# A graph layer on one core: second stage's first loads later, last read-backs into other buffers, sums in front of squares, and a plain tile behind a correction

## The chip, the core and the metric

The kernel runs on one core of a Trainium2 chip. The metric is the device time of one execution in microseconds. TensorE is called PE in the profile, VectorE DVE, ScalarE ACT, GpSimd POOL, and SyncE, which issues most transfers, SP.

## The reference

50,000 nodes with 512 features each, and 75,000 edges: 12,500 drawn ones in both directions and a loop at every node. A node's neighbours are averaged, two products and a bias give `h`, `h` is normalised over all nodes (a batch normalisation), added to `x` after a relu, and each row is normalised once more. All in float32.

```python
summed = jax.ops.segment_sum(x[src], dst, num_segments=n)
cnt = jax.ops.segment_sum(jnp.ones((src.shape[0],), x.dtype), dst, num_segments=n)
aggr = summed / jnp.maximum(cnt, 1.0)[:, None]
h = aggr @ W_l.T + b_l + x @ W_r.T
mu = jnp.mean(h, axis=0)
var = jnp.mean(jnp.square(h - mu), axis=0)
h_norm = (h - mu) * jax.lax.rsqrt(var + EPS) * gamma + beta
...
x = _layernorm(x + relu(h_norm), axis=-1)
```

## The kernel before

Rows are handled in groups of 640, five tiles of 128 rows: 78 whole groups (0 to 77) and a last one, 78, of 80 rows. There are two stages.

**Stage one** writes `h` to `h_scratch` in HBM. Most nodes have no neighbour but themselves, so `h` is first `x` times the sum of both weight matrices. A *plain tile* is that product for 128 rows: `product` (L524 to L526), twelve matmuls, three for each of four slices of the contraction, because every float32 operand is split into a high and a low part. ScalarE makes `x_hi` from `raw` (L728), VectorE `x_lo` (L1045), ScalarE copies the product from bank `pd` to `h_out` (L735), SyncE stores a group (L379).

Nodes with real neighbours need a correction. They are packed 128 to a half, two halves to a *pair*; there are U = 78 pairs. For pair `u`, GpSimd gathers rows (`xe`, `xn`, `xf`, L1331), VectorE forms differences `dd` (L1094), TensorE spreads the extra rows (L613, L614), transposes a difference (L621) and multiplies it by the left weights into bank `pz` (`correction`, L627 to L629, twelve matmuls). ScalarE makes `dT_hi` (L786), VectorE `dT_lo` (L1100), ScalarE scales the product into `zz` (`copy_z`, L793), and GpSimd adds it to `h_scratch` by a scatter (L1379). Both halves use the one bank `pz`, so correction 1 waits until `zz` of half 0 has been copied.

All engines walk the same list of *turns*, u = -2 to 81. A turn holds pair `u`, four or five plain tiles (`tiles_at(u)`; none from turn 75 on), the making of one-hots and slots for pair `u + 2` (`fill_slots`, L600, L603), and sums: group `u - 3` is read back from `h_scratch` into `hs` (`load_sums`, L392, two buffers), VectorE adds it to `acc1` (`take_sums`, L1109), ScalarE squares it in place (L799) and VectorE adds the squares to `acc2` (`take_squares`, L1116). Among the turns 2 to 74, 34 have four tiles. The order in an engine is the order of the code; engines meet at semaphores.

SyncE waits in `load_sums` for the stores of the group, for the scatters of pair `g + 1` (at most 77), and for the squares that last used the buffer. In turn 74, behind the last store, `load_early` issues the loads of the second stage's first three blocks (KEPT = 3).

At the end of stage one TensorE sums the accumulators over the partitions (`sum_columns`, L643) and VectorE and ScalarE turn them into a scale and an offset for each feature (`bn_ready`).

**Stage two** reads `h` and `x` again in blocks of 640 rows, into nine places (NB2 = 9) that lie over the buffers of stage one. GpSimd scales `h` (L1402), VectorE adds the offset (L1243) and forms `y` with its sum (L1248), ScalarE takes squares about the mean (L881) and normalises (`normalise`, L891), SyncE stores (L493). Block `k` is normalised behind the squares of block `k + 1`. `raw` and `x_lo` lie under place 0, `x_hi` under place 1, `h_out` under place 2.

## Time and profile before

| | us |
|---|---|
| median of three runs | 2595.24 |
| lowest, highest | 2591.77, 2596.50 |
| the profiled execution, own time | 2596.68 |
| its span in the trace | 2594.9 |
| TensorE busy | 1757.6 (68% of the span) |
| VectorE busy | 1956.6 (75%) |
| ScalarE busy | 1471.8 (57%) |
| GpSimd busy | 1456.2 (56%) |

The numbers below come from the one profiled execution. Busy shares are means over two stages that have little in common, so they say little; what an engine waits for, and in which stretch, says more. The ends of matmuls are modelled, and one begins before the last is shown as over; the distance between starts is what counts.

### The profile page before, as it was taken

To read this page: it belongs to the slowest core of one execution; us is meant where nothing else is said; L and a number is where in the kernel's file an instruction comes from. 1 tells how busy PE (TensorE), PEld (TensorE's weight loads), DVE (VectorE), ACT (ScalarE), POOL (GpSimd) and SP (SyncE) were. 2 spreads that over 40 slices of the span, in tenths; PEclk is the share of its full clock that TensorE was granted. 3 is DMA by queue.
4 is the path that set the end of the run, shared out by engine and by line. 5 is a ranking of instruction groups with operands and counts; after the bars stand their busy time and mean duration, and the time that the engine had idled before them with its cause. 6 is when DMAs were issued, how large, how long until landed. Compare 5 with 4: busy or idle time off the path is not lost.

```text
span 2594.9 us, 29629 instructions
## 1 busy us (share of the span) xinstructions
PE 1757.6 (68%) x9404; PEld 1415.7 (55%) x9404; DVE 1956.6 (75%) x3451; ACT 1471.8 (57%) x2847; POOL 1456.2 (56%) x700
## 2 busy tenths in 40 slices
PE   7899999999999999999999999996400000000000
PEld 5778778878877887787778778874200000000000
DVE  6745878888877888888788888785688666666666
ACT  4333455545554554454445445542389988888887
POOL 5354555555555555555565555554196655555564
PEclk9999999999999999999999999997755555555555
DMA  5466878887888878888788878877599999999998
GB/s 184 139 211 206 260 250 266 277 253 246 257 263 255 258 246 259 258 255 264 234 262 271 255 243 253 280 240 247 163 410 426 426 426 426 426 412 414 421 421 344
DMA packets 125533, 752.89 MB, mean 290 GB/s; under 512 B 20809, under 2 KB 20809, under 8 KB 65726
## 3 DMA queue, kind: packets, MB, share of 16 engines
q1 hardware_dynamic: 70464, 617.84, 62.1%
q0 software_dynamic: 53664, 132.51, 20.7%
q8 instruction: 77, 1.26, 0.2%
q10 hardware_dynamic: 1246, 0.60, 0.1%
q14 instruction: 82, 0.67, 0.1%
HBM read 515.32 MB, written 246.22 MB: 293 GB/s over the span
## 4 chain that ended last, share of the span: by engine, by line
PE 33%; DMA 32%; issue 9%; DVE 9%; ACT 8%; POOL 7%; SPq 0%; POOLq 0%; ACTq 0%; DVEq 0%
DMA out<-hx 19%; PE pd L524 7%; PE pd L526 7%; PE pd L525 7%; DMA xn<-x,gi 5%; DMA xf<-x,gi 5%; PE pz L627 3%; PE pz L629 3%; PE pz L628 3%; ACT hx L881 3%; POOL xn L1331 2%; ACT hx L891 2%; DVE x_lo L1045 2%; POOL xf L1331 2%; DMA hs<-h_scratch 1%
## 5 line engine op out<-in xcount | busy, mean ns | idle before, releaser
L524 PE MATMUL pd<-wc_hi,x_hi 128*128 128x512 f32 x1564 | 628.8, 402 | 34.8 <-DVE wc_lo L922 17.3
L1379 POOL DMA_INDIRECT h_scratch<-zz,si x156 | 308.8, 1979 | 564.5 <-ACT zz L793 506.9
L735 ACT ACTIVATE h_out<-pd 128x512 f32<-128x512 f32 x391 | 233.6, 597 | 672.3 <-PE pd L526 652.1
L526 PE MATMUL pd<-wc_hi,x_lo 128*128 128x512 f32 x1564 | 614.6, 393 | 0.0
L525 PE MATMUL pd<-wc_lo,x_hi 128*128 128x512 f32 x1564 | 612.9, 392 | 0.0
L1402 POOL TENSOR_TENSOR hx<-hx,scale_b 128x2560 f32<-128x2560 f32 (+2 forms) x91 | 439.4, 4838 | 293.3 <-DMA hx<-h_scratch 251.8
L524 PEld LDWEIGHTS pd<-wc_hi,x_hi 128*128 128x128 f32 x1564 | 295.4, 189 | 98.5 <-issue 29.9
L526 PEld LDWEIGHTS pd<-wc_hi,x_lo 128*128 128x128 f32 x1564 | 295.2, 189 | 64.7
L525 PEld LDWEIGHTS pd<-wc_lo,x_hi 128*128 128x128 f32 x1564 | 295.9, 189 | 57.9
L1331 POOL DMA_INDIRECT xn<-x,gi x156 | 264.9, 1698 | 47.7 <-issue 47.7
L881 ACT ACTIVATE hx<-hx,nm 128x512 f32<-128x512 f32 x391 | 277.1, 710 | 2.8
L891 ACT ACTIVATE hx<-hx,nr,rs 128x512 f32<-128x512 f32 x385 | 278.6, 798 | 0.0
L627 PE MATMUL pz<-wl_hi,dT_hi 128*128 128x512 f32 x624 | 256.5, 411 | 28.9 <-ACT zz L793 20.3
L1331 POOL DMA_INDIRECT xf<-x,gi x156 | 248.7, 1594 | 47.6 <-issue 47.3
L1079 DVE SCALAR_TENSOR_TENSOR xf<-xn,ndeg,xf 128x512 f32<-128x512 f32 x156 | 114.9, 746 | 185.8 <-issue 140.3
L799 ACT ACTIVATE hs<-hs 128x512 f32<-128x512 f32 x391 | 219.1, 621 | 51.1 <-DVE acc L1109 51.1
L628 PE MATMUL pz<-wl_lo,dT_hi 128*128 128x512 f32 x624 | 247.4, 396 | 0.0
L629 PE MATMUL pz<-wl_hi,dT_lo 128*128 128x512 f32 x624 | 246.4, 395 | 0.0
L728 ACT ACTIVATE x_hi<-raw 128x640 fp32r<-128x640 f32 (+1 forms) x316 | 214.1, 724 | 40.7 <-DMA raw<-xT_whole 40.6
L1109 DVE TENSOR_TENSOR acc<-acc,hs 128x2560 f32<-128x2560 f32 (+1 forms) x79 | 220.1, 2786 | 21.7 <-DMA hs<-h_scratch 21.7
L1116 DVE TENSOR_TENSOR acc<-acc,hs 128x2560 f32<-128x2560 f32 (+1 forms) x79 | 220.2, 2787 | 16.0 <-ACT hs L799 16.0
L1045 DVE TENSOR_TENSOR x_lo<-raw,x_hi 128x640 fp32r<-128x640 f32 x280 | 209.4, 808 | 14.7 <-ACT x_hi L728 14.7
(221 smaller groups left out, 2855.0 us busy)
## 6 DMA issues: line engine op xcount, KB each, us to landing
raw<-xT_whole SPq DMA_DIRECT2D x78, 1280.0 KB
h_scratch<-h_out SPq DMA_DIRECT2D x78, 1280.0 KB
hs<-h_scratch SPq DMA_DIRECT2D x78, 1280.0 KB
hx<-x SPq DMA_DIRECT2D x78, 1280.0 KB, 20.7
hx<-h_scratch SPq DMA_DIRECT2D x77, 1280.0 KB, 15.4
out<-hx SPq DMA_DIRECT2D x77, 1280.0 KB, 18.0
xn<-x,gi POOLq DMA_INDIRECT x156
xf<-x,gi POOLq DMA_INDIRECT x156
```

What stands on the lines that cost most here:

```text
L524: pe.matmul(pd[i][0:n, :], hi, wc["hi"][:, kc, :], start=kc == 0, stop=False)
L525: pe.matmul(pd[i][0:n, :], hi, wc["lo"][:, kc, :], start=False, stop=False)
L526: last = pe.matmul(pd[i][0:n, :], lo, wc["hi"][:, kc, :], start=False, stop=kc == KC - 1)
L627: pe.matmul(out_bank[0:n, :], hi, wl["hi"][:, kc, :], start=kc == 0, stop=False)
L628: pe.matmul(out_bank[0:n, :], hi, wl["lo"][:, kc, :], start=False, stop=False)
L629: last = pe.matmul(out_bank[0:n, :], lo, wl["hi"][:, kc, :], start=False, stop=kc == KC - 1)
L881: act.activation(hb[i][0:n, t, :], xb[i][0:n, t, :], ACT.Square, bias=nm2[0:n, k % 4, t:t + 1], accum_out=ssq2[0:n, k % 4, t:t + 1]).then_ ...
L891: act.activation(hb[i][0:n, t, :], xb[i][0:n, t, :], ACT.Identity, bias=nr2[0:n, k % 4, t:t + 1], scale=rs2[0:n, k % 4, t:t + 1]).then_inc ...
L1045: dve.tensor_tensor(x_lo[:, b, kc, 0:n], raw[:, b, kc, 0:n], x_hi[:, b, kc, 0:n].bitcast(F32), ALU.subtract).then_inc(s_xld, 1)
L1331: return pool.indirect_dma_start(out=table if scatter else out, out_offset=by if scatter else None, in_=out if scatter else table, in_offs ...
L1379: pool.indirect_dma_start(out=h_dram[:, :], out_offset=by, in_=zz[:, h, :], in_offset=None, bounds_check=N + 2 * P - 1, oob_is_err=True, c ...
L1402: pool.tensor_tensor(hb[i][0:n, a:b], hb[i][0:n, a:b], scale_b[0:n].unsqueeze(1).to_broadcast([n, b - a, D]), ALU.mult).then_inc(s_mul, 1)
```

## The change

Five things, in the order of the program.

- SyncE no longer issues the first loads of stage two in turn 74. It issues two blocks (EARLY2 = 2) in turn 77, once all gathers of the last pair have landed, and four more (up to KEPT = 6) after the last read-back, once TensorE has finished all corrections. Places are handed out in another order, so that the place over `h_out` comes seventh.
- The read-backs of groups 76 and 77 go into the two halves of `h_out`, and each of the last three has a semaphore of its own; they no longer wait for squares.
- From turn 78 on VectorE takes the sums of a group ahead of the squares of the group before.
- In turns with four plain tiles TensorE does the fourth behind correction 0 and not ahead of it.
- In stage two block 0 is normalised at once, ahead of the squares of block 1.

```diff
@@ the places
-        KEPT = 3
+        EARLY2, KEPT = 2, 6
         hx = s2("hx", [P, NB2, 2, TG, D], F32)
-        hb = [hx[:, i, 0] for i in range(NB2)]
-        xb = [hx[:, i, 1] for i in range(NB2)]
+        places = (0, 1, 3, 4, 5, 6, 2, 7, 8)
+        hb = [hx[:, i, 0] for i in places]
+        xb = [hx[:, i, 1] for i in places]
@@ new
+        def sums_of(g):
+            return h_out[:, g % 2] if isinstance(g, int) and G - 2 <= g < G else hs[:, g % 2]
+
+        def read_back(g):
+            return s_sl_end[g - G + 2] if isinstance(g, int) and g >= G - 2 else s_sl[g % 2]
@@ SyncE, load_sums
-                if g >= 2:
-                    sp.wait_ge(s_a2, g - 1)
-                sp.dma_start(part_of(hs[:, b], g), group_of(h_dram, g)).then_inc(s_sl[b], 16)
+                if G - 2 <= g < G:
+                    sp.wait_ge(s_st[0], stored(G))
+                    sp.wait_ge(s_st[1], stored(G - 1))
+                elif g >= 2:
+                    sp.wait_ge(s_a2, g - 1 if g < G else G - 3)
+                sp.dma_start(part_of(sums_of(g), g), group_of(h_dram, g)).then_inc(read_back(g), 16)
@@ SyncE, the turns
                         if t == tiles_in(g) - 1:
                             after_group(g, g % 2)
-                        if g == G:
-                            load_early()
                     if sums_at(u + 1) is not None:
                         load_sums(sums_at(u + 1))
+                    if u == U - 1:
+                        sp.wait_ge(s_ge, 16 * U)
+                        for h in range(2):
+                            sp.wait_ge(s_gn[h], 16 * U)
+                            sp.wait_ge(s_gf[h], 16 * U)
+                        sp.wait_ge(s_dm, TG * G + 1)
+                        load2(0, EARLY2)
+                sp.wait_ge(s_z, 2 * U)
+                load2(EARLY2, KEPT)
             sp.wait_ge(s_done, 1)
-            for k in range(KEPT, NB2 - 1):
-                load2_h(k)
-                load2_x(k)
+            load2(KEPT, NB2 - 1)
@@ TensorE, the turns
-                    plain(3)
+                    if len(tiles) == TG:
+                        plain(3)
                     if a is not None:
                         correction(a, 0)
-                    plain(4)
+                    plain(3 if len(tiles) < TG else 4)
                     if u + 2 < U:
                         fill_slots(u + 2)
@@ ScalarE, stage two (VectorE's invert in the same way)
-                if k >= 1 and not by_vector(k - 1):
+                if k == 0:
+                    normalise(0)
+                if k >= 2 and not by_vector(k - 1):
                     normalise(k - 1)
@@ VectorE, the turns
-                    if sums_at(u - 1) is not None:
+                    if u < U and sums_at(u - 1) is not None:
                         take_squares(sums_at(u - 1))
...
                     if sums_at(u) is not None:
                         take_sums(sums_at(u))
+                    if u >= U:
+                        take_squares(sums_at(u - 1))
```

TensorE in turn 66, which has four tiles, from transposition 1 on (bank `p7`), before. `pd0` is the fourth plain tile, `pz` with `dT_hi0` correction 0, `psl` the slots, `pz` with `dT_hi1` correction 1; of each block of twelve matmuls the first stands here.

```order
L621 MATMUL p7<-ident,dd 128x128 [waits dT_lo_ready,differences_ready]
L621 MATMUL p7<-ident,dd 128x128 x3
L524 MATMUL pd0<-wc_hi,x_hi 128x512 [waits h_copied]
...
L627 MATMUL pz<-wl_hi,dT_hi0 128x512 [waits z_copied,dT_lo_ready]
...
L600 MATMUL psl<-vals,hot 128x6 [waits slots_copied,one_hots_built]
L600 MATMUL psl<-vals,hot 128x6 x12
L603 MATMUL psl<-valsx,hotx 128x4 x10
L627 MATMUL pz<-wl_hi,dT_hi1 128x512 [waits z_copied,dT_lo_ready]
```

The same stretch of TensorE after the change.

```order
L636 MATMUL p7<-ident,dd 128x128 [waits dT_lo_ready,differences_ready]
L636 MATMUL p7<-ident,dd 128x128 x3
L642 MATMUL pz<-wl_hi,dT_hi0 128x512 [waits z_copied,dT_lo_ready]
...
L539 MATMUL pd0<-wc_hi,x_hi 128x512 [waits h_copied]
...
L615 MATMUL psl<-vals,hot 128x6 [waits slots_copied,one_hots_built]
L615 MATMUL psl<-vals,hot 128x6 x12
L618 MATMUL psl<-valsx,hotx 128x4 x10
L642 MATMUL pz<-wl_hi,dT_hi1 128x512 [waits z_copied,dT_lo_ready]
```

Correction 0 and the fourth tile have changed places; nothing else in the turn has.

ScalarE in the same turn, after the change, from `dT_hi` of half 1 on. Apart from line numbers it reads so before too: the copy of the fourth tile (`h_out<-pd0`) stands ahead of `xe_hi` and of `zz` of correction 0.

```order
L802 ACTIVATE dT_hi1<-p7 128x512 [waits z_summed,differences_transposed]
L751 ACTIVATE h_out<-pd0 128x512 [waits h_summed]
L796 ACTIVATE xe_hi<-xe 128x512 [waits extras_spread,extras_gathered]
L809 ACTIVATE zz<-pz,wgt 128x512 [waits z_added0,weights_ready,z_summed]
L815 ACTIVATE hs<-hs 128x512 [waits sums_taken]
L815 ACTIVATE hs<-hs 128x512 x2
L809 ACTIVATE zz<-pz,wgt 128x512 [waits z_added1,weights_ready,z_summed]
```

Nothing moved on this engine, while one of the things it waits for did.

SyncE's queue before, from the last group's store in turn 74 on: three blocks of `hx`, then the read-backs into `hs` of groups 72 to 74 (four more stand behind them).

```order
L379 DMA h_scratch<-h_out 80x512 [waits h_copied]
L399 DMA hx<-h_scratch 128x2560 [waits h_stored0,h_stored1,h_copied,h_summed]
L403 DMA hx<-x 128x2560
L399 DMA hx<-h_scratch 128x2560
...
L392 DMA hs<-h_scratch 128x2560 [waits z_added1,squares_taken,z_added0,h_stored0]
L392 DMA hs<-h_scratch 128x2560 [waits z_added1,squares_taken,z_added0,h_stored1]
```

SyncE's queue after, from the read-back of group 74 on.

```order
L406 DMA hs<-h_scratch 128x2560 [waits z_added1,squares_taken,z_added0,h_stored0]
L406 DMA hs<-h_scratch 128x2560 [waits z_added1,squares_taken,z_added0,h_stored1]
L413 DMA hx<-h_scratch 128x2560 [waits rows_gathered1,neighbours_gathered1,neighbours_gathered0,h_summed,rows_gathered0,extras_gathered]
L417 DMA hx<-x 128x2560
...
L406 DMA h_out<-h_scratch 128x2560 [waits h_stored0,z_added1,h_stored1,z_added0] x2
L406 DMA hs<-h_scratch 80x512 [waits z_added1,squares_taken,z_added0,h_stored0]
L413 DMA hx<-h_scratch 128x2560 [waits z_summed]
L417 DMA hx<-x 128x2560
```

The loads of `hx` have moved behind four of the seven read-backs (two blocks) and behind all seven (four blocks).

## Rows read from the trace of the kernel before

**Rows 1.** The page, busy tenths and GB/s in 40 slices of the span.
```profile
PE   7899999999999999999999999996400000000000
...
GB/s 184 139 211 206 260 250 266 277 253 246 257 263 255 258 246 259 258 255 264 234 262 271 255 243 253 280 240 247 163 410 426 426 426 426 426 412 414 421 421 344
```

**Rows 2.** TensorE's waits, 450 to 1740 us: us in total, times, longest.
```profile
PE pz L627 <- ACT zz L793: 12.1, 28, 1.5
...
PE pe L613 <- issue: 1.0, 6, 0.2
```

**Rows 3.** Timeline of TensorE, turn 66: start, us, what, wait before it.
```profile
1591.47 0.48 PE L524 MATMUL pd<-wc_hi,x_hi 128*128 128x512 f32 x1
...
1594.32 0.39 PE L627 MATMUL pz<-wl_hi,dT_hi 128*128 128x512 f32 x1
...
1598.07 0.47 PE L627 MATMUL pz<-wl_hi,dT_hi 128*128 128x512 f32 x1 [0.30 <-ACT zz L793]
...
1600.89 0.39 PE L613 MATMUL pe<-xe_hi,spread 128*128 128x512 f32 x1
```

**Rows 4.** Timeline of ScalarE, turn 66.
```profile
1588.60 1.36 ACT L728 ACTIVATE x_hi<-raw 128x640 fp32r<-128x640 f32 x2
...
1594.52 0.60 ACT L735 ACTIVATE h_out<-pd 128x512 f32<-128x512 f32 x1 [2.12 <-PE pd L526]
1595.01 0.62 ACT L780 ACTIVATE xe_hi<-xe 128x512 fp32r<-128x512 f32 x1
1597.24 0.69 ACT L793 ACTIVATE zz<-pz,wgt 128x512 f32<-128x512 f32 x1 [1.60 <-PE pz L629]
```

**Rows 5.** Timelines, turns 17, 19, 66: fourth tile's start, low part of difference 0.
```profile
552.75 0.48 PE L524 MATMUL pd<-wc_hi,x_hi 128*128 128x512 f32 x1
...
554.93 0.68 DVE L1100 TENSOR_TENSOR dT_lo<-px,dT_hi 128x512 fp32r<-128x512 f32 x1
...
595.89 0.48 PE L524 MATMUL pd<-wc_hi,x_hi 128*128 128x512 f32 x1
...
596.71 0.68 DVE L1100 TENSOR_TENSOR dT_lo<-px,dT_hi 128x512 fp32r<-128x512 f32 x1
...
1590.48 0.69 DVE L1100 TENSOR_TENSOR dT_lo<-px,dT_hi 128x512 fp32r<-128x512 f32 x1 [0.47 <-ACT dT_hi L786]
```

**Rows 6.** TensorE around two waits; stretches with granted clock, DMA share, GB/s last.
```profile
792.23 0.68 PE L627 MATMUL pz<-wl_hi,dT_hi 128*128 128x512 f32 x1 [1.50 <-ACT zz L793]
...
796.64 0.40 PE L613 MATMUL pe<-xe_hi,spread 128*128 128x512 f32 x1
...
1025.82 0.47 PE L627 MATMUL pz<-wl_hi,dT_hi 128*128 128x512 f32 x1 [1.52 <-ACT zz L793]
...
780.00:800.00 20.00, 18.50 (x99) 15.03 (x98) 13.23 (x18) 8.52 (x15) 13.09 (x6) 0.91 0.82 272
1015.00:1035.00 20.00, 18.48 (x104) 14.84 (x103) 15.67 (x23) 9.84 (x18) 11.04 (x7) 1.00 0.90 280
1580.00:1602.00 22.00, 21.70 (x120) 17.84 (x119) 19.68 (x36) 11.77 (x21) 11.13 (x7) 1.00 0.87 279
```

**Rows 7.** The seam: chain of waits (first row), timelines, one stretch.
```profile
1774.70 29.31 DMA hs<-h_scratch
...
1804.04 2.83 DVE L1109 TENSOR_TENSOR acc<-acc,hs 128x2560 f32<-128x2560 f32 x1 [21.69 <-DMA hs<-h_scratch]
...
1809.97 1.56 POOL L1379 DMA_INDIRECT h_scratch<-zz,si  x1 [16.41 <-DVE si L1069]
...
1844.44 0.33 SPq L392 DMA_DIRECT2D hs<-h_scratch  x1
...
1862.21 2.71 ACT L799 ACTIVATE hs<-hs 128x512 f32<-128x512 f32 x5 [5.63 <-DVE acc L1109]
...
1869.06 0.69 DVE L1116 TENSOR_TENSOR acc<-acc,hs 80x512 f32<-80x512 f32 x1 [0.69 <-ACT hs L799]
...
1910.00:1920.00 10.00, 0.00 (x0) 0.00 (x0) 9.97 (x32) 9.90 (x23) 10.00 (x3) 0.50 0.95 365
```

More of the change, by code:

```diff
@@ L265, in bass_sage_batchnorm_residual_layernorm_kernel @@
         s_sl = [sem(f"h_loaded{b}") for b in range(2)]
+        s_sl_end = [sem(f"h_end_loaded{i}") for i in range(3)]
         s_a1, s_sq, s_a2 = sem("sums_taken"), sem("squares_ready"), sem("squares_taken")
@@ L403, in load2_x, with load2 @@
                 sp.dma_start(part_of(xb[i], k), group_of(x, k)).then_inc(s_x2[i], 16)
-            def load_early():
-                sp.wait_ge(s_dm, TG * G + 1)
-                sp.wait_ge(s_ev, TG * G + 1)
-                sp.wait_ge(s_st[0], stored(G))
-                sp.wait_ge(s_st[1], stored(G - 1))
-                for k in range(KEPT):
+            def load2(first, end):
+                for k in range(first, end):
                     load2_h(k)
@@ L466, in _ @@
                 correct(G)
-                load_early()
+                sp.wait_ge(s_done, 1)
+                load2(0, KEPT)
             with sp.Else():
@@ L798, in square @@
                     act.wait_ge(s_a1, g + 1)
-                act.activation(hs[0:n, g % 2, t, :], hs[0:n, g % 2, t, :], ACT.Square).then_inc(s_sq, 1)
+                act.activation(sums_of(g)[0:n, t, :], sums_of(g)[0:n, t, :], ACT.Square).then_inc(s_sq, 1)
             act.wait_ge(s_flag, 1)
@@ L1104, in take_sums @@
                 n, t = rows_in(g), tiles_in(g)
-                dve.wait_ge(s_sl[g % 2], stored(g))
+                dve.wait_ge(read_back(g), stored(g) if g < G - 2 else 16)
                 dve.wait_ge(s_clear, 1)
@@ L1108, in take_sums @@
                     dve.wait_ge(s_a1, g)
-                dve.tensor_tensor(acc1[0:n, 0:t], acc1[0:n, 0:t], hs[0:n, g % 2, 0:t], ALU.add).then_inc(s_a1, 1)
+                dve.tensor_tensor(acc1[0:n, 0:t], acc1[0:n, 0:t], sums_of(g)[0:n, 0:t], ALU.add).then_inc(s_a1, 1)
             def take_squares(g):
@@ L1115, in take_squares @@
                     dve.wait_ge(s_a2, g)
[L1116 removed]
+                dve.tensor_tensor(acc2[0:n, 0:t], acc2[0:n, 0:t], sums_of(g)[0:n, 0:t], ALU.add).then_inc(s_a2, 1)
             dve.wait_ge(s_flag, 1)
@@ L1275, in _ @@
                     sum_y(k, t)
-                if k >= 1:
+                if k == 0:
+                    invert(0)
+                if k >= 2:
                     invert(k - 1)
```

5 lines of the change are left out of this document (1 added, 4 removed).

## The prediction, made before the kernel had run

> **What bounds the kernel now.** I read the page first: its forty slices show TensorE at nine tenths or more up to about 1770 us and then nothing, and the transfers at 410 to 426 GB/s from about 1870 us to the end [rows 1]. So there are two stages and a seam. In stage one TensorE sets the pace: between 450 and 1740 us its waits are six kinds, 28 us in 1290, the largest the 28 waits for the scaled copy `zz` with 12.1 us and the least 1.0 us [rows 2]. In stage two the transfers set the pace. The seam, 1770 to 1915 us, is a chain of waits with no engine busy. A microsecond saved on ScalarE or VectorE is worth nothing in either stage, but a microsecond in which TensorE stands still in stage one is lost whole. I therefore looked first for what the change does to TensorE's order, which its title does not mention, and then at the seam.
>
> **Part one: the fourth tile behind the first correction.** A turn `u` of the loop handles one pair of corrections and the next four or five plain tiles; 34 turns have four, 43 have five. Five-tile turns keep their order. In a four-tile turn TensorE now does transposition 1, correction 0, the fourth tile, the slots, correction 1, where it did the fourth tile before correction 0. ScalarE's order stays: copy of the fourth tile (`h_out`), `xe_hi`, `zz` of correction 0. Correction 1 needs that `zz`, since both use bank `pz`. Before, the fourth tile's copy was long done when correction 0 ended; now the copy waits for a product that ends later than correction 0, and `zz` stands behind it.
>
> Worked out on turn 66. Before, the fourth tile starts at 1591.47, where transposition 1 ends, correction 0 at 1594.32, and correction 1 at 1598.07, after 0.30 of waiting [rows 3]. ScalarE takes up `zz` at 1597.24, when correction 0 is out, and TensorE goes on 0.83 later [rows 3, 4]. After, the two blocks change places, so the fourth tile ends where correction 0 ended. ScalarE starts `h_out` at 1597.24, needs 0.49 for it (1594.52 to 1595.01) and about 0.54 for `xe_hi` (0.62 less the tenth by which neighbours overlap) [rows 4], takes up `zz` at 1598.27, and correction 1 starts at 1599.10: **1.03 us later**. Times 34 turns: 35 us. VectorE's work on `xe` is delayed alike and stays just in time for the next turn.
>
> When the fourth tile is a group's tile 1 or 2, two `x_hi` conversions follow its copy and also stand ahead of `zz`: 1.36 us for the pair [rows 4], 1.26 after overlap, in 14 turns: 18 us.
>
> Correction 0 now comes straight behind transposition 1 and needs `dT_lo` of half 0. In turn 66 that ends at 1591.17 and the transposition at 1591.47: no wait [rows 3, 5]. In turn 17 VectorE has a group's `x_lo` ahead of it and finishes at 555.61, while the fourth tile starts at 552.75: 2.9 us, which that tile covered before. In turn 19 it is 597.39 against 595.89: 1.5 us [rows 5]. Read off so, 19 turns have such a lateness and together 40 us.
>
> Sum 93 us. The 28 old waits above their usual 0.30 (12.1 less 28 times 0.30, [rows 2]) are already in the old times and come off: 89. Some is recovered: a TensorE that waits lets VectorE and the gathers catch up, so the other five kinds of waits, 16 us, fall away, and turn 17's lateness shrinks a little. I allow 20 us for both; the rest is **+69**. Bounds: 53 us if no `dT_lo` is ever late and 89 with no recovery.
>
> **The clock.** The new standstills are longer than the old. At 792.23 TensorE had waited 1.50 us with only the tiny slot products before it; the granted clock of that stretch is 0.91, and the correction that follows takes until 796.64, 4.41 us, where turn 66's takes 2.82 [rows 3, 6]. At 1025.82 it had waited 1.52 us and the clock stayed at 1.00 [rows 6]. So a fall to the lower level (1.2 instead of 2.4 GHz) costs 1.6 us and comes at some waits of 1.5 us. The change makes 53 standstills: 34 at correction 1 of about 1.4 us, 2.7 in the fourteen turns with `x_hi`, and 19 at correction 0. I count 24 falls, the long ones and some of the short: **+38**. From below it is 0, from above 85 (53 times 1.6).
>
> The Trainium skill bears on this ("TensorE: Matmul & The Clock Gate", section "A second HAM failure mode: psum-queue depth-cycling"): short idles between groups of matmuls that come often enough make the clock swing between half and full. By that rule already the small waits of before should do it; the stretch of 22 us around turn 66 with its 0.30 shows a clock of 1.00 [rows 6], so here size decides and not number. By the rule the clock would fall at nearly every new wait; that is the second rival.
>
> **Part two: the seam.** Before, SyncE issues six loads of 1.31 MB ahead of the read-back of group 72, which is issued at 1774.70 and lands 29.31 us later; VectorE stands 21.69 us [rows 7]. After, that read-back goes first and VectorE needs it at 1782.4, when it is long there: the stall goes. What is late next is the pair chain. `zz` of pair 75 waited for VectorE's sums through ScalarE's squares, so its scatter went out at 1809.97 [rows 7]. Without that, and with `xe` gathered through a free queue, correction 1 of pair 75 ends near 1792 and its scatter goes at about 1793, an estimate between 1791 and 1795: 17 us earlier. From there to the last scatter the steps stay as they were.
>
> Two blocks (5.2 MB, 12.3 us at 426 GB/s) are now loaded between the last gathers and the last scatters. They share the transfer engines with the scatters, which must have landed before the last three read-backs are issued. Cost between 0 and 6 us; I take 2. A read-back was issued at 1844.44 when the last scatter had landed [rows 7]. From there came rounds of 8.3 us, ScalarE's 2.71 of squares and 5.63 of waiting for VectorE [rows 7]: sums 2.8, squares 2.7, squares added 2.8, each behind the one before. With three buffers the read-backs follow one another and the next sums run while ScalarE squares: 5.5 us a round. From 1844.44 to the end of the last addition, 1869.75 [rows 7], was 25.3 us, and is now about 5 for landing plus 15.4. But the column sums of the squares wait for group 77's squares, which are now 1.3 us closer to the end, so 3.6 us remain. Seam: 17 plus 3.6 less 2, **-19**.
>
> **Part three: stage two.** Three more blocks are there early, and block 0 is normalised and stored about 8 us sooner. I cost both at nothing. The store that starts the steady stream is block 1's, behind GpSimd's block 2, which hangs on the batch statistics alone. Before it, the transfers already had a gap (0.95 busy, 365 GB/s at 1910 to 1920, [rows 7]); all nine blocks were in. Loads that come earlier make that gap longer, and only that. If I were wrong, the bound is three blocks of two loads, 18 us at 426 GB/s.
>
> **Sum.** The profiled execution's span is 2594.9, its own time 2596.7, the median 2595.2. Span: 2594.9 + 69 + 38 - 19 = 2682.9; with the 0.3 us by which the median stands above the span, **2683**.
>
> **Rivals.**
> 1. The waits come, the clock does not fall (for: 1025.82; against: 792.23). 2595.2 + 69 - 19 = 2645. Chance 0.22.
> 2. The clock falls at nearly every wait, as the skill's rule would have it, and nothing is recovered: 2595.2 + 89 + 70 - 19 = 2735. Chance 0.08. The mechanism is the same wait; the price is 1.6 us each, from the correction at 792.23.
> 3. Not slower: TensorE does not set stage one's pace but VectorE and the gathers behind it do, so the moved tile's wait falls into time that was idle anyway, while the 12.1 us of old `zz` waits are gone. 2595.2 - 12 - 19 = 2564. Against it stands that TensorE had so few waits [rows 2]. It decides in favour of faster once more than 88 of the 107 us are absorbed. Chance 0.07.
> 4. Absorbed in part, so that waits and seam cancel within 5 us: chance 0.03.
>
> **How the numbers follow.** The forecast has 0.60. Its own range is 2655 to 2715: 53 to 80 us of waits, 20 to 60 of clock, 13 to 25 of seam. To leave out no more than two in ten the range takes in most of rival 1 and stops short of rivals 2 and 3: 2632 to 2725. A measurement can tell about 0.2%, 5 us. Slower 0.60 + 0.22 + 0.08 = 0.90, same 0.03, faster 0.07.
>
> **What would show it.** Right: in the trace of after the waits of TensorE at `pz` for ScalarE's `zz` go from 12 us to 50 or more, a wait for `dT_lo` of some 30 us appears, four-tile turns take 1 to 5 us longer, the granted clock dips below 1.00 in many stretches, and stage two starts 70 to 110 us later, though the distance from the last four-tile turn to the first normalised block shrinks by about 19 us. Wrong: if stage one ends before about 1780 us, rival 3 holds; if it ends near 1840 with the clock at 1.00, rival 1; if stage two lasts less than before by over 5 us, part three was wrong.

## The result and the profile after

| | before | after |
|---|---|---|
| median, us | 2595.87 | 2705.25 |
| lowest, highest of four runs each | 2591.77, 2598.57 | 2700.10, 2709.44 |
| span of the profiled execution | 2594.9 | 2698.1 |
| TensorE's waits on `pz`, 450 to 1740 us | 13.3 | 87.8 |
| start of turn 75, the first without tiles | 1772.91 | 1893.56 |
| from there to the end of the span | 822.0 | 804.5 |

The change makes the kernel slower by 4.2% (ratio 1.0422, 95% interval 1.0402 to 1.0442). The two last rows tell the story in two numbers: stage one became 120.7 us longer, and seam and stage two together 17.5 us shorter. The forecast was 2683, with 107 and 19 for the two.

On the page of after, busy tenths, granted clock and GB/s in 40 slices, TensorE's row has eights where it had nines [rows 1]:

```profile
PE   7899989989999999899899999999510000000000
...
PEclk9999999999999999999999999999755555555555
...
GB/s 177 156 193 224 251 188 263 263 196 241 236 243 239 223 247 253 243 230 256 235 223 237 257 220 228 263 244 205 216 363 420 426 426 426 426 426 426 413 421 342
```

A tenth is too coarse for the clock. The stretch that [rows 2] cover, with the granted clock and the DMA share behind the busy times (it was 1.00 and 0.82 before), and TensorE's waits in the same stretch (us in total, times, longest):

```profile
450.00:1740.00 1290.00, 1199.23 (x6442) 977.79 (x6441) 980.45 (x1403) 591.14 (x1029) 659.57 (x397) 0.97 0.77 238
...
PE pz L642 <- ACT zz L809: 46.4, 26, 2.6
PE pz L642 <- DVE dT_lo L1118: 41.4, 15, 4.4
PE p L636 <- DVE dd L1112: 2.4, 4, 0.8
PE pd L539 <- issue: 0.4, 1, 0.4
```

The six kinds of waits of [rows 2] have become four. The first went from 12.1 to 46.4 us and a second, for `dT_lo`, from 1.2 to 41.4. All others together fell from 14.4 to 2.8: while TensorE stands still, what it would else have waited for gets ready. (The same 1290 us hold fewer turns in after, so the true growth is larger; the table by turns below has it.)

**Turn 66, the `zz` wait.** TensorE's timeline, to be held against [rows 3], then ScalarE's, against [rows 4]:

```profile
1701.16 0.48 PE L642 MATMUL pz<-wl_hi,dT_hi 128*128 128x512 f32 x1
...
1704.01 0.39 PE L539 MATMUL pd<-wc_hi,x_hi 128*128 128x512 f32 x1
...
1708.77 0.57 PE L642 MATMUL pz<-wl_hi,dT_hi 128*128 128x512 f32 x1 [1.30 <-ACT zz L809]
...
1713.18 0.40 PE L628 MATMUL pe<-xe_hi,spread 128*128 128x512 f32 x1
```
```profile
1706.93 0.60 ACT L751 ACTIVATE h_out<-pd 128x512 f32<-128x512 f32 x1 [4.83 <-PE pd L541]
1707.42 0.62 ACT L796 ACTIVATE xe_hi<-xe 128x512 fp32r<-128x512 f32 x1
1707.94 0.68 ACT L809 ACTIVATE zz<-pz,wgt 128x512 f32<-128x512 f32 x1
```

Correction 0 is at 1701.16, the fourth tile at 1704.01. ScalarE, idle for 4.83 us, copies that tile as soon as it is there, then `xe_hi`, and only then `zz`, on which correction 1 waits 1.30 us in place of 0.30. The forecast had 1.03 more; it is 1.00. Then the clock: from the second product behind the wait on they follow one another at 0.43 us instead of 0.23, and the correction takes 4.41 us (1708.77 to 1713.18) where turn 66 had taken 2.82 [rows 3].

**Turn 41, the `dT_lo` wait.** VectorE's timeline, then TensorE's first product of correction 0 and the tile that follows it:

```profile
1121.58 0.75 DVE L1097 SCALAR_TENSOR_TENSOR xf<-xn,ndeg,xf 128x512 f32<-128x512 f32 x1 [6.08 <-issue]
...
1127.93 3.04 DVE L1063 TENSOR_TENSOR x_lo<-raw,x_hi 128x640 fp32r<-128x640 f32 x4
1130.89 2.81 DVE L1134 TENSOR_TENSOR acc<-acc,hs 128x2560 f32<-128x2560 f32 x1
1133.63 0.68 DVE L1118 TENSOR_TENSOR dT_lo<-px,dT_hi 128x512 fp32r<-128x512 f32 x1
```
```profile
1134.36 0.50 PE L642 MATMUL pz<-wl_hi,dT_hi 128*128 128x512 f32 x1 [3.43 <-DVE dT_lo L1118]
...
1138.65 0.54 PE L539 MATMUL pd<-wc_hi,x_hi 128*128 128x512 f32 x1
```

`x_lo` of a whole group (3.04) and the addition of the squares (2.81) stand ahead of `dT_lo` on VectorE. That was so before, and the fourth tile covered it. But VectorE is also late as a whole: it stood 6.08 us ahead of `xf`. The profile names no releaser there; the instruction waits for gathered rows. In turn 40, GpSimd's last gather and the read-back that SyncE issues, in after and then in before:

```profile
1110.04 0.33 SPq L406 DMA_DIRECT2D hs<-h_scratch  x1
...
1111.13 3.63 POOL L1353 DMA_INDIRECT xf<-x,gi  x1 [0.30 <-issue]
```
```profile
1038.21 1.17 POOL L1331 DMA_INDIRECT xf<-x,gi  x1 [0.30 <-issue]
...
1042.06 0.33 SPq L392 DMA_DIRECT2D hs<-h_scratch  x1
```

Before, the gather went out 9.58 us into turn 40 and 3.85 ahead of the read-back; after, 12.01 into the turn and 1.09 behind it, and it occupied GpSimd for 3.63 us in place of 1.17. The turn itself is shorter, 21.65 us in place of 23.00; TensorE had waited 0.85 us in it and no longer does.

**All turns.** I added up the distance between the starts of neighbouring turns, TensorE's waits in them, and, as time lost to the lower clock, the excess over 2.85 us of each correction or tile that took more than 0.6 us longer than that (each is one fall). In turns 3 to 74:

| | turns | total before | after | waits before | after | lost to the clock before | after | falls |
|---|---|---|---|---|---|---|---|---|
| four tiles | 33 | 647.3 | 798.1 | 14.4 | 115.0 | 1.6 | 45.3 | 1, then 28 |
| five tiles | 39 | 878.3 | 844.4 | 19.8 | 0.0 | 3.1 | 0.0 | 2, then 0 |

The five-tile turns, which the change leaves alone, became 34 us shorter; that is the recovery. Of the 151 us that the four-tile turns grew, 100.6 are waits and 43.7 clock.

**The seam of after.** In order of time: GpSimd's scatter that answers to the one at 1809.97 in [rows 7], SyncE's first early load, the last scatter, the last read-backs, the first sums that they bring, GpSimd's first work of stage two.

```profile
1912.80 1.56 POOL L1401 DMA_INDIRECT h_scratch<-zz,si  x1 [2.02 <-ACT zz L809]
...
1934.54 0.33 SPq L413 DMA_DIRECT2D hx<-h_scratch  x1
...
1942.54 1.56 POOL L1401 DMA_INDIRECT h_scratch<-zz,si  x1 [2.27 <-ACT zz L809]
...
1953.16 0.83 SPq L406 DMA_DIRECT2D h_out<-h_scratch  x2
...
1958.56 2.83 DVE L1127 TENSOR_TENSOR acc<-acc,h_out 128x2560 f32<-128x2560 f32 x1 [12.90 <-DMA h_out<-h_scratch]
...
1987.39 3.71 POOL L1424 TENSOR_TENSOR hx<-hx,scale_b 128x512 f32<-128x512 f32 x3 [43.29 <-DVEq L1256]
```

Counted from the start of turn 75, the scatter of [rows 7] at 1809.97 stood at 37.06 us and stands at 19.24, 17.8 earlier. The last scatter came 17.8 earlier too (66.76, now 48.98), the last read-backs 11.9 earlier (71.53, now 59.60), and GpSimd's stage two 16.0 earlier (109.78, now 93.83). The read-backs wait for the last scatter to land: 4.8 us before, 10.6 now.

### The profile page after: what moved, and what is told of

Its sections match the earlier page's. It is cut to its first block, busy times and chain, and to the rows that moved or that the text cites. A ratio compares the mean times of both kernels' runs of the same rounds, so it can differ in the third digit from the quotient of the medians.

```text
span 2698.1 us, 29630 instructions
## 1 busy us (share of the span) xinstructions
PE 1792.7 (66%) x9404; PEld 1451.1 (54%) x9404; DVE 1958.2 (73%) x3451; ACT 1467.0 (54%) x2847; POOL 1432.6 (53%) x700
## 3 DMA queue, kind: packets, MB, share of 16 engines
q8 instruction: 77, 1.26, 0.2%
## 4 chain that ended last, share of the span: by engine, by line
PE 44%; DMA 28%; ACT 9%; DVE 7%; issue 7%; POOL 4%; SPq 0%; POOLq 0%; ACTq 0%; DVEq 0%
DMA out<-hx 18%; PE pd L539 8%; PE pd L541 8%; PE pd L540 8%; PE pz L642 5%; PE pz L644 5%; PE pz L643 5%; DMA xn<-x,gi 3%; ACT hx L897 3%; ACT hx L907 2%; DMA raw<-xT_whole 2%; DMA xf<-x,gi 2%; DVE x_lo L1063 2%; DMA h_scratch<-zz,si 1%; ACT zz L809 1%
## 5 line engine op out<-in xcount | busy, mean ns | idle before, releaser
L1401 POOL DMA_INDIRECT h_scratch<-zz,si x156 | 317.2, 2034 | 734.1 <-ACT zz L809 677.8
L642 PE MATMUL pz<-wl_hi,dT_hi 128*128 128x512 f32 x624 | 274.5, 440 | 122.7 <-ACT zz L809 63.8
L1353 POOL DMA_INDIRECT xn<-x,gi x156 | 247.0, 1583 | 47.7 <-issue 47.4
L644 PE MATMUL pz<-wl_hi,dT_lo 128*128 128x512 f32 x624 | 265.4, 425 | 0.0
L643 PE MATMUL pz<-wl_lo,dT_hi 128*128 128x512 f32 x624 | 264.6, 424 | 0.0
L815 ACT ACTIVATE hs<-hs 128x512 f32<-128x512 f32 x381 | 213.7, 623 | 7.5 <-DVE acc L1127 7.5
L1127 DVE TENSOR_TENSOR acc<-acc,hs 128x2560 f32<-128x2560 f32 (+1 forms) x77 | 214.5, 2785 | 3.4 <-DMA hs<-h_scratch 3.4
L1134 DVE TENSOR_TENSOR acc<-acc,hs 128x2560 f32<-128x2560 f32 (+1 forms) x77 | 214.6, 2786 | 0.6 <-ACT hs L815 0.5
```

The lines of the kernel that those rows point to most:

```text
L642: pe.matmul(out_bank[0:n, :], hi, wl["hi"][:, kc, :], start=kc == 0, stop=False)
L643: pe.matmul(out_bank[0:n, :], hi, wl["lo"][:, kc, :], start=False, stop=False)
L644: last = pe.matmul(out_bank[0:n, :], lo, wl["hi"][:, kc, :], start=False, stop=kc == KC - 1)
L1353: return pool.indirect_dma_start(out=table if scatter else out, out_offset=by if scatter else None, in_=out if scatter else table, in_offs ...
L1401: pool.indirect_dma_start(out=h_dram[:, :], out_offset=by, in_=zz[:, h, :], in_offset=None, bounds_check=N + 2 * P - 1, oob_is_err=True, c ...
```

## The experiments

Times are medians; the ratio is to the kernel before on the same chip, with its 95% interval. A difference between two kernels is the difference of their ratios times 2594 us, since not all ran in one session.

### The tile's place: the change without it, and it alone

```diff
  x1_order_back: the changed kernel, with
-                    if len(tiles) == TG:
-                        plain(3)
+                    plain(3)
                     if a is not None:
                         correction(a, 0)
-                    plain(3 if len(tiles) < TG else 4)
+                    plain(4)
```
x2_tile_alone is the kernel before with the same lines the other way round.

> The changed kernel, with TensorE's tiles of a four-tile turn in the order of the kernel before (fourth tile, correction 0, nothing, correction 1). Theory (the tile's new place costs about 120 us in stage one, and the seam gives about 17.5 back): 2595.9 - 17.5 = about 2578, which is 125 to 130 us under the changed kernel. In the trace the waits of the four-tile turns are near 14 us in place of 115, and the granted clock of stage one is near that of the kernel before. Rival (the loss comes from the new places of the loads and read-backs, and the tile is innocent): about 2700, as the changed kernel.

> The kernel before, with the one edit of TensorE's order: in a four-tile turn the fourth tile comes behind correction 0. Theory (the loss and the gain lie in different stages and add up): 2595.9 + 120.7 = about 2717, so slower than the changed kernel by the seam's 17 us. Rival (the tile costs nothing by itself): about 2596. A third outcome, about 2705, would say that the seam's gain was made by something in the tile's move.

x1_order_back: 2585.43, ratio 0.9970 (0.9955 to 0.9985). x2_tile_alone: 2716.06, ratio 1.0489 (1.0460 to 1.0519), where the theory said 2717. The tile's place alone makes the loss: it costs 127 us when it is put into the kernel before, and taking it out of the changed one gives 117 back. In x2's trace turn 75 begins at 1886.10, 113 us late, with 25 falls of the clock in four-tile turns. TensorE's waits of x1_order_back, 450 to 1740 us, are those of [rows 2] again:

```profile
PE pz L642 <- ACT zz L808: 14.7, 28, 2.4
...
PE pz L642 <- DVE dT_lo L1117: 1.5, 5, 0.3
```

One part missed. The seam alone was to give 17.5 us, and x1_order_back gains 7.8 (3.9 to 11.7). Its profiled span, 2578.1, has 5 of its 17 us from a stage one that happened to be shorter, and 11.6 behind the start of turn 75. What became of the rest is told with the seam, below.

### ScalarE's share: `zz` first

```diff
  x3_zz_first: the changed kernel, ScalarE's turn
-                    plain(tiles[3:4])
+                    if len(tiles) == TG:
+                        plain(tiles[3:4])
                     if pair_at(u + 1) is not None:
                         extras_high(u + 1)
                     if a is not None:
                         copy_z(a, 0)
-                    plain(tiles[4:])
+                    plain(tiles[4:] if len(tiles) == TG else tiles[3:4])
```

> The changed kernel, with one edit on ScalarE: in a four-tile turn it copies the half of z that correction 1 multiplies ahead of the fourth tile's copy, not behind it. Theory (both standstills of TensorE have a cause of their own, and the clock falls with each): the waits of correction 1 on that copy, 54 us in the sum, go; those of correction 0 on dT_lo, 44 us, stay; about half of the 28 falls of the clock (some 20 us) go with them. 2705 - 54 - 20 = about 2630, range 2615 to 2655. Rival A (the dT_lo waits shrink too, since VectorE gets its tiles sooner): under 2600. Rival B (what is taken off one wait comes back in the other, because a turn is as long as VectorE's and ScalarE's chain): above 2680.

2619.74, ratio 1.0106 (1.0076 to 1.0136), 82 us under the changed kernel. Its waits, 450 to 1740 us:

```profile
PE pz L642 <- DVE dT_lo L1119: 44.2, 16, 4.1
PE pe L628 <- DVE xe_lo L1103: 2.5, 6, 0.4
PE p L636 <- DVE dd L1113: 2.3, 6, 0.8
```

The `zz` wait has left this list and the `dT_lo` wait is where it was, 44.2 for 41.4: two waits with two causes, and the theory holds within 10 us. The falls went from 28 to 13.

It shows more: VectorE's lateness does not come from the late `zz`. In turn 41, with `zz` on time, VectorE stands at `xf` and TensorE waits for `dT_lo` no less than in the changed kernel:

```profile
1079.76 0.75 DVE L1098 SCALAR_TENSOR_TENSOR xf<-xn,ndeg,xf 128x512 f32<-128x512 f32 x1 [6.37 <-issue]
```
```profile
1092.64 0.80 PE L642 MATMUL pz<-wl_hi,dT_hi 128*128 128x512 f32 x1 [3.84 <-DVE dT_lo L1119]
```

So it is in turns 8, 19, 30, 41, 52 and 63, the turns whose fourth tile is a group's tile 0 (turn 74, the seventh, has no such wait): TensorE waits 3.8 to 5.0 us there, in after 3.4 to 4.5. Ahead of each, in both kernels, the last gather stands 1.1 us behind the read-back; in the kernel before it stands 2.4 to 3.9 ahead of it.

### The clock's share: standstills filled with work

```diff
  x4_busy_waits: the changed kernel, TensorE's turn
+                    def busy(n):
+                        for _ in range(n):
+                            pe.matmul(pe_[:], wc["hi"][:, 0, 0:P], wc["hi"][:, 0, :], start=True, stop=True)
...
+                    if len(tiles) == 4 and a is not None and tiles[3][1] in (0, 1, 2):
+                        busy(6)
                     if a is not None:
                         correction(a, 0)
...
                         fill_slots(u + 2)
+                    if len(tiles) == 4 and a is not None:
+                        busy(10 if tiles[3][1] in (1, 2) else 5)
                     if a is not None:
                         correction(a, 1)
```

> The changed kernel, with products of TensorE that nobody reads put into its standstills: 6 ahead of correction 0 in the kinds of turn that waited there, 5 or 10 ahead of correction 1. They only keep the engine working; the waits' causes are as they were. Theory (of the 120 us, about 45 are the clock falling to half after a standstill, the rest are the waits themselves): the granted clock of stage one is back near 1.00 and the time is 35 to 45 us under the changed kernel, about 2665, less what the products overrun the waits. Rival (the falls fall beside the wait and cost nothing of their own): 2705 or more.

2661.69, ratio 1.0266 (1.0245 to 1.0286), 40 us under the changed kernel with more work on TensorE, not less. ScalarE's and VectorE's orders are as they were, so the causes of the waits are too; only TensorE is busy until they end. The stretch of 450 to 1740 us, the clock third from last:

```profile
450.00:1740.00 1290.00, 1262.77 (x6831) 1025.58 (x6830) 999.98 (x1425) 604.64 (x1053) 679.30 (x407) 0.99 0.79 245
```

0.99 where the changed kernel has 0.97; in the four-tile turns 5 falls in place of 28, and 9.3 us lost in place of 45.3. So the clock is a cost of its own, some 45 us, of which 36 went here; the rest of the tile's 117 is waits. This separates the two terms of the forecast, 69 and 38.

### VectorE's share: `dT_lo` first as well

```diff
  x12_both_first: x3_zz_first, VectorE's turn
+                    if p is not None:
+                        difference_low(p, 0)
                     x_lows(1)
                     if u < U and sums_at(u - 1) is not None:
                         take_squares(sums_at(u - 1))
-                    if p is not None:
-                        difference_low(p, 0)
                     x_lows(2)
```

> x3_zz_first (the changed kernel with TensorE's new order, and z copied first), and on VectorE the low part of difference 0 taken ahead of the group's x_lo and the squares, in every turn. In x3_zz_first TensorE still waited 54 us for dT_lo and the clock fell 13 times. Theory (dT_lo of half 0 is late because x_lo and the squares stand ahead of it on VectorE, 3.0 and 2.8 us): those waits shrink to under 15 us, the falls to a few, and the time is 2620 - 40 - 15 = about 2565. Rival (VectorE itself is late in these turns, since the gathers land late, so the order inside the turn matters little): above 2600. A third outcome, x_lo now late for the next turn's tiles, would show as waits of TensorE's tiles on x_lo.

2575.58, ratio 0.9938 (0.9920 to 0.9956): 44 us under x3_zz_first. The rival said over 2600; it fell. The theory's number, 2565, is missed by 10. Its waits, 450 to 1740 us:

```profile
PE pd L539 <- issue: 14.6, 7, 2.9
PE px L636 <- DVE dd L1113: 8.1, 7, 1.7
PE pe L628 <- DVE xe_lo L1103: 5.9, 11, 0.5
PE p L636 <- DVE dd L1113: 3.7, 9, 0.8
PE pz L642 <- ACT zz L809: 0.8, 1, 0.8
```

`dT_lo` is gone from the list. With TensorE's new order and the two engines that feed it put in the same order, the four-tile turns take 637.0 us, 10 less than before the change, with no fall of the clock. The tile's new place was not wrong by itself: it was moved on one engine of three. But the five-tile turns took 886.1 us, 8 more than before, with 34.3 us of waits in place of 19.8 (on `issue` ahead of a tile, and on `dd`) and five falls in place of two, 8.5 us in place of 3.1. I tried whether VectorE's new order does that there:

```diff
  x13_four_only: x12_both_first, with
-                    if p is not None:
+                    early = len(tiles_at(u)) < TG
+                    if p is not None and early:
                         difference_low(p, 0)
...
+                    if p is not None and not early:
+                        difference_low(p, 0)
                     x_lows(2)
```

> x12_both_first, with VectorE's new order (low part of difference 0 first) in turns of fewer than five tiles alone. In x12_both_first the four-tile turns took 637 us in place of 647, but the five-tile turns 886 in place of 878, with 34 us of waits. Theory A (VectorE's order there makes them wait): the five-tile turns come down by 10 us or more and the time is about 2565. Theory B (TensorE, when it gains in the four-tile turns, runs into the loads and gathers, and gives the gain back in whatever turn follows): five-tile turns stay near 885 and the time at 2575, within 3 us.

2576.17, ratio 0.9927 (0.9914 to 0.9940). Theory B: four-tile turns 634.0, five-tile turns 889.9 with 35.9 us of waits, and the start of turn 75 at 1771.73, where it was 1769.88 in x12_both_first and 1772.91 in the kernel before. What TensorE gains in one kind of turn is handed back in the other. That loads and gathers are what it then runs into is read from the waits' names, not shown by a run of its own.

### ScalarE's order with the old order of TensorE

x8_zz_first_old_order is x1_order_back with the ScalarE diff above.

> x1_order_back, with ScalarE's copy of z for correction 1 taken ahead of the fourth tile's copy in four-tile turns. TensorE had there, in each four-tile turn, one wait of 0.30 us for that copy. Theory (TensorE's order with a tile between is right, and ScalarE's order is free to be changed): these go, 10 us in the sum, and nothing comes in their place: 2585 - 10 = about 2575. Rival (the fourth tile's copy, x_lo and with it dT_lo come later, and the 10 us are given back): 2585 or more.

2575.95, ratio 0.9930 (0.9910 to 0.9949), 10 us under x1_order_back. The number came, the reason did not. The waits of 0.30 us are still in every kind of four-tile turn (28 waits for `zz`, now 8.6 us, all near 0.30): nothing lies between the corrections but the slots, so they measure the way from one correction over the copy to the next. Two other things moved. In turns whose fourth tile is a group's tile 1, two `x_hi` conversions no longer stand ahead of `zz`; those seven turns fell from 20.98 to 19.56 us each, 10 in the sum (the traces scatter here: 20.25 in the kernel before, 20.04 in x10_both), but the five-tile turns rose by 12 and the profiled stage one kept nothing (turn 75 starts at 1770.36, in x1_order_back's profile at 1767.73). And the seam with stage two became 6 us shorter (804.3, after 810.4), which may be most of the 10 and goes with something worth seeing. In x1_order_back SyncE issues a read-back at 1762.48 and VectorE then stands 7.45 us until the gathered `xf` is there; in x8 the last tile's copy is 3.3 us later against turn 75's start, the store and the read-back behind it go out at 1768.42, and VectorE stands 2.16. The two rows of each:

```profile
1762.48 0.54 SPq L406 DMA_DIRECT2D hs<-h_scratch  x1
...
1771.74 0.75 DVE L1096 SCALAR_TENSOR_TENSOR xf<-xn,ndeg,xf 128x512 f32<-128x512 f32 x1 [7.45 <-issue]
```
```profile
1768.42 10.41 SPq L406 DMA_DIRECT2D hs<-h_scratch  x2
...
1769.07 0.75 DVE L1097 SCALAR_TENSOR_TENSOR xf<-xn,ndeg,xf 128x512 f32<-128x512 f32 x1 [2.16 <-issue]
```

The gathers had been issued alike (the last at 1760.70 in x1_order_back and 1763.31 in x8, 2.84 us each on GpSimd's queue); they landed within 8.2 us beside the read-back and 2.9 us without it. The other traces agree: in the five with the read-back 1.4 to 2.0 us behind the gather (x1, x5, x6, x7, x9) the gather landed 6.7 to 8.5 us after its end on GpSimd's queue, in the other nine within 4.6. In the changed kernel, too, the late copies of turn 74 keep the read-back (1888.46) behind the last gather (1883.28), and VectorE goes through both `xf` without a wait at 1889.33.

The missing part of x1_order_back's seam goes with this. From turn 75's start to the end, the traces of x1, x6 and x7, with the stall, have 809.8 to 813.5 us, and those of the changed kernel, x3, x4, x8, x12 and x13, with early loads, buffers and order of sums as in x1 but no stall, 802.4 to 805.2. So some 6 of the changed kernel's 17.5 us come with the order that costs 120 elsewhere. How the stall becomes 6 us is only in part seen: the last scatter is 2.0 us later in x1 than in the changed kernel, and the other 4 lie behind it.

### The seam: early loads

```diff
  x5_no_early: x1_order_back, with
-        EARLY2, KEPT = 2, 6
+        EARLY2, KEPT = 0, 6
```

> The kernel with the old tile order (x1_order_back), but no block of stage two loaded ahead of the last scatters: all six wait for the last read-back. In x1_order_back the last scatter starts at 51.0 us after turn 75 and the last read-backs are issued 11.0 us later; in the kernel before these were 4.8 us. Theory (the two early blocks, 12 us of transfers, lie in front of the scatters' landing): read-backs 4 to 6 us after the last scatter, and the time 4 to 6 us under x1_order_back's 2585, about 2580. Rival (the landing depends on something else, the scatter's own rows say): 11 us stay, and the time is x1_order_back's or a little above.

2581.81, ratio 0.9952 (0.9934 to 0.9969), 4.7 us under x1_order_back, but the two intervals overlap, and x6_block0_as_before below, whose edit lies in stage two and moves no later store, has the same ratio. The time gained is therefore not shown; the landing is. The last scatter and the last read-backs of x5, then those of x1_order_back:

```profile
1831.46 1.56 POOL L1400 DMA_INDIRECT h_scratch<-zz,si  x1 [0.31 <-issue]
...
1836.92 0.83 SPq L406 DMA_DIRECT2D h_out<-h_scratch  x2
```
```profile
1818.74 2.66 POOL L1400 DMA_INDIRECT h_scratch<-zz,si  x1 [2.26 <-ACT zz L808]
...
1829.69 0.83 SPq L406 DMA_DIRECT2D h_out<-h_scratch  x2
```

5.5 us against 11.0: the two early blocks cost 5.5 us of landing. All traces fall in two sets: 4.6 to 5.5 us where no block is loaded there (before, x2, x5, x10), 10.3 to 12.4 where two are. (The last scatter itself was 2 us later in x5, by the turn before it, so the read-backs gained 3.5.) x10_both adds the same edit to x8_zz_first_old_order.

> x8_zz_first_old_order (old order of TensorE, ScalarE's copy of z first in four-tile turns) with no block of stage two ahead of the last scatters, as in x5_no_early. If the two gains lie at different places they add up: 2576 less 4 to 5, about 2571. Rival (x8's gain was in part the shorter seam, whose first scatter came 5 us earlier than in x1_order_back, and the landing no longer decides): 2576, as x8.

2574.66, ratio 0.9926 (0.9909 to 0.9943), level with x8's 0.9930. The read-backs come 5.7 us earlier (53.86 us after turn 75's start, after 59.57) and GpSimd's stage two 5.6 earlier, but the end of the span only 1.7 earlier: here stage two took 714.2 us and in x8 710.3. The gain does not add up; why stage two takes it back is open.

### The seam: buffers

```diff
  x9_old_buffers: x1_order_back, with
         def sums_of(g):
-            return h_out[:, g % 2] if isinstance(g, int) and G - 2 <= g < G else hs[:, g % 2]
+            return hs[:, g % 2]
...
         def load_sums(g): (SyncE)
-                if G - 2 <= g < G:
-                    sp.wait_ge(s_st[0], stored(G))
-                    sp.wait_ge(s_st[1], stored(G - 1))
-                elif g >= 2:
-                    sp.wait_ge(s_a2, g - 1 if g < G else G - 3)
+                if g >= 2:
+                    sp.wait_ge(s_a2, g - 1)
```

> x1_order_back, with the last read-backs in the two old buffers, so that each waits for the squares before it; the loads stay where the changed kernel has them and the order of sums and squares too. Theory (of the seam's gain, the part after the last scatter is 3 us and all the rest is the read-back that no longer stands behind loads): 3 us above x1_order_back, about 2588, and the start of GpSimd's stage two 38 us after the last read-back is issued in place of 35.6. Rival A (the buffers bring the seam's whole gain): 2592 or more. Rival B (they bring nothing): 2585.

2592.48, ratio 0.9994 (0.9983 to 1.0006): not to be told from the kernel before, and 6.2 us over x1_order_back. The number is rival A's. The moved loads do bring the last scatter 14.6 us forward (52.14 us after turn 75's start, before 66.76), but the landing takes 5.8 of that, and the rest goes in the rounds at the end. VectorE's sums of groups 76 and 77:

```profile
1839.80 2.82 DVE L1123 TENSOR_TENSOR acc<-acc,hs 128x2560 f32<-128x2560 f32 x1 [12.89 <-DMA hs<-h_scratch]
1842.54 2.82 DVE L1130 TENSOR_TENSOR acc<-acc,hs 128x2560 f32<-128x2560 f32 x1
1851.04 2.83 DVE L1123 TENSOR_TENSOR acc<-acc,hs 128x2560 f32<-128x2560 f32 x1 [5.67 <-DMA hs<-h_scratch]
```

Group 77's read-back is asked for when squares have been added out of its buffer, at 1845.36, and lands 5.7 us later. In the kernel before the next sums never waited for a read-back here. From the last read-backs to GpSimd's first work it is 38.2 us before, 44.3 in x9 and 35.6 in x1_order_back.

This is not the price of the buffers by themselves. x9 keeps the new order, sums ahead of squares from turn 78 on. ScalarE had squared group 75 by 1826.65, and VectorE stood idle from 1826.92 to 1839.80 (12.89 us), but the order makes it take group 76's sums first and only then the squares that free the buffer. In the old order they would be added in that idle time. So the new order without the new buffers costs some 6 us between the last read-backs and GpSimd (44.3, after 38.2), and order and buffers together gain 2.6 (35.6, after 38.2), near the 3.6 of the forecast. The moved loads have the last read-backs issued 8.8 us earlier in x9 (62.69, before 71.53); what they would be worth with both the old order and the old buffers no run shows.

### Stage two

```diff
  x7_two_kept: x1_order_back, with
-        EARLY2, KEPT = 2, 6
+        EARLY2, KEPT = 2, 2

  x6_block0_as_before: x1_order_back, with (ScalarE; VectorE's invert alike)
-                if k == 0:
-                    normalise(0)
-                if k >= 2 and not by_vector(k - 1):
+                if k >= 1 and not by_vector(k - 1):
                     normalise(k - 1)
```

> x1_order_back, with only two blocks, not six, loaded before the batch sums are out; the other four wait for the signal that stage one is done. Theory (part three of the prediction: what is loaded early only widens a gap in the transfers, which the store of block 1 ends): the time is x1_order_back's, 2585, within 3 us. Rival (transfers are the bound of the whole stage two, so four blocks of 2.6 MB that come earlier are worth up to 25 us at 426 GB/s): 2595 to 2610.

> x1_order_back, with block 0 of stage two normalised where the kernel before has it, not ahead of block 1's squares. Theory (part three: that block's earlier store, some 18 us ahead of the next one, moves no later one): 2585, as x1_order_back, within 4 us. Rival (the store that goes out early takes its 12 us off the steady stream): 2592 or more.

x7: 2584.94, ratio 0.9967 (0.9954 to 0.9979), as x1_order_back's 0.9970: four blocks loaded early or not make no difference. x6: 2581.38, ratio 0.9952 (0.9933 to 0.9970), the same or a little faster. SyncE's first two stores of x1_order_back, then of x6:

```profile
1879.27 0.34 SPq L508 DMA_DIRECT2D out<-hx  x1
...
1897.18 0.34 SPq L508 DMA_DIRECT2D out<-hx  x1
```
```profile
1892.05 0.34 SPq L508 DMA_DIRECT2D out<-hx  x1
...
1901.86 0.34 SPq L508 DMA_DIRECT2D out<-hx  x1
```

From the start of turn 75, block 0's store is at 111.5 in one and 119.5 in the other, block 1's at 129.5 and 129.3. The second is the one from which the steady stream runs, and it does not move.

## Why the prediction was right, and where its terms were off

The sign, the mechanism and the place were right, and 2705 lies in the range. Step by step, in the profiled execution:

- **`zz` wait, +1.03 and +1.26 us a turn.** 1.00 and 1.25: the waits are 1.30 and 2.55 us. x3_zz_first takes them away with one edit on ScalarE.
- **`dT_lo` wait, 40 us in 19 turns.** The mis-sized term: 50.7 us in 18 turns. The waits of four-tile turns grew by 100.6 us where the two terms less the old waits made 89. The error lies in the turns whose fourth tile is a group's tile 0: I read off 1.5 us (turn 19, [rows 5]) and six of the seven waited 3.4 to 4.5. The lateness was read from the trace of before as if VectorE kept its place relative to TensorE. It did not: in turn 41 it began its first difference 2.75 us behind TensorE's start (1123.52, 1120.77), and in the kernel before 0.66 (1052.29, 1051.63). The late `zz` is not the reason, since VectorE is as late in x3_zz_first. What the traces show ahead of each such wait is a five-tile turn that had lost its waits (21.6 to 21.8 us long, before 22.5 to 26.0), with the last gather 12.0 to 12.2 us into it (before 9.5 to 11.6) and no longer ahead of the read-back. In x12_both_first, where no `dT_lo` wait is left, the gather is 3.1 to 3.9 us ahead of the read-back again in all six turns and VectorE begins 0.65 to 0.92 us behind TensorE. So part of the recovery in one turn seems to come back as a wait in the next. That reading has no run of its own, and why GpSimd's queue is slower there stays open.
- **Recovery, -20 us.** The other mis-sized term, in the other direction: -34, the five-tile turns' 878.3 to 844.4. I had counted the listed waits alone (16 us), where all 19.8 went with 3.1 us of clock, and the rest was in gaps too short to be listed.
- **Clock, 24 falls, +38 us.** 28 falls, +43.7 us; x4_busy_waits, which leaves 5 falls, gives 37 us of stage one and 40 of the time back. Rival 1 (no falls) and rival 2 (a fall at nearly every wait) both fell. In the 13 turns with nothing but a wait of 1.30 us the clock fell five times; in the 20 turns with a wait of 2.55 us or two waits, 23 times. The Trainium skill's rule ("TensorE: Matmul & The Clock Gate", section "A second HAM failure mode: psum-queue depth-cycling"), frequent short idles make the clock swing, agrees with the new standstills in kind, and the section gives no size of idle. The small waits of before, 28 of 0.43 us on average, left the clock at 1.00 [rows 2, 6].
- **Stage one, +107.** +120.7: four-tile turns +150.8, five-tile turns -33.9, the few turns outside the count +3.8. That 107 came so near is in part luck: the new waits were put 12 us too low and the recovery 14, and these two misses cancel.
- **Seam, -19.** -17.5, right in the sum and in part by luck. I had 17 for the earlier scatter, 2 of cost for its landing and 3.6 for the last rounds. In the trace the last scatter is 17.8 us earlier, its landing takes 5.9 longer (the bound of 6 and not the 2 I took), the way from the read-backs to GpSimd is 4.0 shorter, and stage two 1.5. With the old order of the tile (x1_order_back) the same four are 15.8, 6.2, 2.6 and -0.6, in all 11.6: the other 6 come with the slowed turn 74, which the forecast did not have.
- **Part three at nothing.** Confirmed by x6 and x7.
- **Rival 3, TensorE doesn't set the pace.** Refuted for a loss, as turn 75's 120.7 us show, but true for a gain: x8, x12 and x13 all take waits out of the four-tile turns and reach turn 75 at 1770 to 1772 us, within the 1765 to 1778 of the kernels whose tiles and `zz` stand as before.

Of the 22 us between 2683 and 2705, then, 14 are stage one's and 1.5 the seam's; the other 7 are that the median stands 7.2 above the profiled span, where I had allowed 0.3. The profiled execution was the fastest of its four.

The best version found, x10_both, runs in 2574.66 us, 0.74% under the kernel before; x8_zz_first_old_order, x12_both_first and x13_four_only cannot be told from it.

## What to carry to other kernels

Where several engines go through the same list of tiles in one agreed order, a move on one of them is a move on all: look for the instruction that now stands ahead of what the moved work releases, on each engine that serves it. Size a lateness from a trace only if the late engine will keep its place against the one that waits: here 1.5 us read off became 3.4 to 4.5. And a small transfer on the critical way, a gather or a scatter, should not be issued beside a bulk one: with 1.3 to 5 MB moved to either side of it, it landed some 5 us sooner each time. What that is worth in the whole kernel was less clear: the runs gained 0 to 6 us.

## What the runs showed of the hardware

A fall of TensorE's clock from 2.4 to 1.2 GHz cost 1.6 us on average (28 falls, 45.3 us) and came after standstills of as little as 1.30 us, but not after all of them (5 of 13). It began with the first products behind the wait in some turns and some products later in others: in turn 66 at the correction's second product, in turn 41 at its sixth. Products that nobody reads, put in the place of the standstills, took 23 of 28 falls away and made the kernel 40 us faster. From the start of the last scatter of 128 rows to the read-back that waits for it, it was 4.6 to 5.5 us without bulk loads beside it (four traces) and 10.3 to 12.4 with two blocks of them (ten traces). The last gather landed within 4.6 us of its end on GpSimd's queue (nine traces), and in 6.7 to 8.5 with a read-back of 1.3 MB issued 1.4 to 2.0 us behind it (five traces).
